# A Mamba-style conv layer on one core: a third conv tap on ScalarE, an accumulating transfer, and ScalarE's products placed behind two decays

## What is computed

```python
# layer 0, DI = 1536 channels, 4 states, R = 48
xs = gn(x) @ in_proj_w.T                       # 768 -> 1536 channels
xs = depthwise_conv3x3(xs, conv_w) + conv_b    # nine taps per channel
u  = xs * sigmoid(xs)
dt, Bs, Cs = split(u @ x_proj_w.T, [R, R + 4])
delta = softplus(dt @ dt_w + dt_b)
dA  = exp(delta[..., None] * A)                # "decays", one per state
dBu = (delta * u)[..., None] * Bs
states = scan(s[t] = dA[t] * s[t-1] + dBu[t])  # along the 4096 positions
y = sum_n(states_n * Cs_n) + D_param * u
y = layernorm(y) * ln_g + ln_b
x = x + y @ out_proj_w.T                       # 1536 -> 768 channels
# layer 1: gn, a 768x768 product, token-statistics attention, a 768x768 product, residual
```

## Time and profile before

| | |
|---|---|
| median of 3 runs | 3728.86 us (3728.01 to 3731.64) |
| the profiled execution: its own time, its span | 3728.46 us, 3726.7 us |
| busy over the span: PE, DVE, ACT, POOL | 3406.2, 2914.2, 2353.8, 2344.5 us |
| 100 to 255 us: conv without scans (PE, DVE, ACT, POOL busy) | 129.75, 81.62, 65.20, 36.70 us of 155 |
| 255 to 2612 us: conv and scans together | 2168.66, 2223.89, 1822.68, 2075.28 us of 2357 |
| 2612 to 2800 us: the tail of layer 0 | 163.86, 123.70, 86.14, 125.30 us of 188 |
| 2800 to 3726.7 us: layer 1 | 893.69, 439.29, 362.81, 104.92 us of 926.7 |

### The profile page before, as it was taken

The page is one execution under the profiler, slowest core; times in us unless marked ns, Lnnn a source line. Parts: engine busy times, 40 slices in busy tenths (PEclk is TensorE's granted clock), DMA queues, the critical chain, the costliest instruction groups (busy, mean ns, idle before and its releaser), DMA issues. The chain is left out here.

```text
span 3726.7 us, 39056 instructions
## 1 busy us (share of the span) xinstructions
PE 3406.2 (91%) x10696; PEld 1733.7 (47%) x10696; DVE 2914.2 (78%) x4082; ACT 2353.8 (63%) x4095; POOL 2344.5 (63%) x1557
## 2 busy tenths in 40 slices
PE   4876799999999999999999999998798999999999
PEld 4432233333333344333333333333235877777787
DVE  4469999999999979999999999999754346566532
ACT  1357777887778757777877778787535556543211
POOL 0149888989889878898988888899850001112211
PEclk7887899999999999999999999999898999999999
DMA  7244455555556544555555555554643223356664
GB/s 284 89 140 109 103 131 139 158 141 146 136 142 157 149 122 122 147 141 140 157 144 146 136 141 150 145 156 113 165 98 115 66 71 111 118 189 211 206 200 153
DMA packets 217034, 529.85 MB, mean 142 GB/s; under 512 B 24728, under 2 KB 45784, under 8 KB 213872
## 3 DMA queue, kind: packets, MB, share of 16 engines
q1 hardware_dynamic: 173808, 376.32, 31.8%
q0 software_dynamic: 43008, 151.02, 18.6%
HBM read 346.11 MB, written 80.48 MB: 114 GB/s over the span
## 5 line engine op out<-in xcount | busy, mean ns | idle before, releaser
L564 PE MATMUL p_in<-xn,win_v 128*128 128x512 f32 (+1 forms) x2304 | 1064.9, 611 | 102.9 <-ACT halo L747 64.6
L580 PE MATMUL p_op<-uy,wout_ring 128*128 128x512 f32 x2160 | 1020.1, 622 | 83.7 <-DVE x_res L952 83.5
L917 DVE TENSOR_TENSOR_SCAN p_da<-p_da,state,g_ring 128x512 f32<-128x512 f32 x672 | 827.1, 1276 | 110.4 <-ACT p_da L706 74.7
L889 POOL TENSOR_TENSOR g_ring<-du,B_bc 128x2048 f32<-128x2048 f32 x192 | 870.6, 4534 | 17.3 <-DMA B_bc<-bc_scratch 2.4
L938 DVE SCALAR_TENSOR_TENSOR p_cv<-win_v,conv_w,p_cv 128x512 f32<-128x512 f32 x960 | 722.7, 753 | 88.0 <-ACT p_cv L768 67.0
L564 PEld LDWEIGHTS p_in<-xn,win_v 128*128 128x128 f32 x2304 | 443.1, 197 | 697.5 <-issue 697.5
L580 PEld LDWEIGHTS p_op<-uy,wout_ring 128*128 128x128 f32 x2160 | 413.4, 198 | 680.4 <-issue 568.3
L706 ACT ACTIVATE p_da<-delta,A 128x512 f32<-128x512 f32 x768 | 499.4, 682 | 12.6 <-ACT state L711 0.2
L923 DVE TENSOR_TENSOR g_ring<-p_da,C_bc 128x512 f32<-128x512 f32 x768 | 486.7, 675 | 0.0
L1366 PE MATMUL banks<-x_split,w_split 128*128 128x512 f32 x1152 | 459.2, 399 | 11.9 <-DVE x_split L1569 6.5
L1368 PE MATMUL banks<-x_split,w_split 128*128 128x512 f32 x1152 | 450.8, 391 | 0.0
(11 more groups left out here) (213 smaller groups left out, 4261.1 us busy)
## 6 DMA issues: line engine op xcount, KB each, us to landing
g_ring<-g_ring POOLq DMA_DIRECT2D x192, 512.0 KB, 5.5
win_v<-in_win SPq DMA_DIRECT2D x192, 384.0 KB, 3.1
wout_ring<-wout_scratch SPq DMA_DIRECT2D x184, 384.0 KB, 4.0
x_ring<-x_scratch SPq DMA_DIRECT2D x192, 256.0 KB, 2.7
q_scratch<-q_ring POOLq DMA_DIRECT2D x96, 256.0 KB, 2.5
x_split<-q_scratch SPq DMA_DIRECT2D x96, 256.0 KB, 3.4
out<-x_ring POOLq DMA_DIRECT2D x96, 256.0 KB, 2.9
x_res<-in_x SPq DMA_DIRECT2D x90, 256.0 KB, 4.6
```

The costliest lines, as they stand in the source:

```text
L564: last = nc.tensor.matmul(p_in[:, 0:n], WR[:, i % NW, t, :], XN[:, t, off:off + n], start=(t == 0), stop=(t == XT - 1))
L580: last = nc.tensor.matmul(p_op[:], OR[:, e % NO, k - h * HALF, :], ucol(c * K + k), start=(k == 0), stop=(k == K - 1))
L889: nc.gpsimd.tensor_tensor(G[:, i % NG], DU[:].unsqueeze(1).broadcast_to([P, NS, N]), BB[:], ALU.mult).then_inc(s_dbu, 1)
L917: nc.vector.tensor_tensor_scan(bank, bank, G[:, i % NG, n, :], init, ALU.mult, ALU.add)\
```

## The change

A third of the conv's products goes from DVE to ACT: tap (2, 0). DVE is left with five taps, three between its two pairs of scans and two at the slot's end. ACT makes three products (`conv_part` has three parts now), and all three stand behind the decays of states 2 and 3, no longer between the centre tap and `keep_state`. POOL adds product 1 onto product 0 with an accumulating transfer in SBUF, which it issues behind the big product with B (L889 of before) once ACT has made product 1 of the tile; its first addition in the next slot waits for that transfer (`s_cf`), and its second one takes product 2. The number of POOL's additions stays. Two semaphores of the layer norm are joined into one, which changes no order. Core of the diff:

```diff
-        CT = sb("conv_part", [P, 2, N])
+        CT = sb("conv_part", [P, 3, N])
@@
-        TAPS = [(dy, dx) for dy in range(3) for dx in range(3) if (dy, dx) not in ((1, 1), (2, 1), (2, 2))]
+        TAPS = [(dy, dx) for dy in range(3) for dx in range(3) if (dy, dx) != (1, 1) and dy < 2]
@@ ScalarE
                 def product(i, n):
-                    wait(act, s_conv, 2 * (i - 1) + n + 1)
-                    nc.scalar.activation(rows(CT[:, n]), win_view(i, 2, 1 + n), ACT.Copy,
-                                         scale=cwt[:, i % K, 7 + n:8 + n]).then_inc(s_ct, 1)
+                    if n == 0:
+                        wait(act, s_conv, 2 * i - 1)
+                    elif n == 1:
+                        wait(act, s_cf, 16 * i)
+                    else:
+                        wait(act, s_conv, 2 * i)
+                    nc.scalar.activation(rows(CT[:, n]), win_view(i, 2, n), ACT.Copy,
+                                         scale=cwt[:, i % K, 6 + n:7 + n]).then_inc(s_ct, 1)
@@
-                    if b is not None:
-                        product(b, 0)
                     i = tile(S, L_SCAN)
                     if i is not None:
                         act.wait_ge(s_du, i + 1)
                         nc.scalar.activation(ucol(i), ucol(i), ACT.Copy, scale=Dp[:, i % K:i % K + 1])\
                           .then_inc(s_skip, 1)
-                    if b is not None:
-                        product(b, 1)
@@
                         decay(i, 2)
                         decay(i, 3)
+                    if b is not None:
+                        product(b, 0)
+                        product(b, 1)
+                        product(b, 2)
                     if S % K == 0 and S < NT:
                         load_norm(S // K)
@@ GpSimd
                     if b is not None:
-                        pool.wait_ge(s_ct, 2 * b + 1)
+                        pool.wait_ge(s_cf, 16 * (b + 1))
                         pool.wait_ge(s_tap, len(TAPS) * (b + 1))
                         nc.gpsimd.tensor_tensor(ucol(b), ucol(b), CT[:, 0], ALU.add).then_inc(s_conv, 1)
-                        pool.wait_ge(s_ct, 2 * b + 2)
+                        pool.wait_ge(s_ct, 3 * b + 3)
                         pool.wait_ge(s_conv, 2 * b + 1)
-                        nc.gpsimd.tensor_tensor(ucol(b), ucol(b), CT[:, 1], ALU.add).then_inc(s_conv, 1)
+                        nc.gpsimd.tensor_tensor(ucol(b), ucol(b), CT[:, 2], ALU.add).then_inc(s_conv, 1)
@@ behind the product with B
+                    t = tile(S, L_CONV)
+                    if t is not None:
+                        pool.wait_ge(s_ct, 3 * t + 2)
+                        nc.gpsimd.dma_start(CT[:, 0], CT[:, 1], accum_op=ALU.add).then_inc(s_cf, 16)
```

19 lines of the change are left out of this document (9 added, 10 removed).

## The result

Four runs of the changed kernel took 3851.54 to 3858.97 us, median **3855.04 us**; four of the kernel before 3728.01 to 3731.64, median 3729.62. The ratio is 1.0336, 95% interval [1.0318, 1.0354]: 125 us slower, where 95 was forecast. That is 32 us above the likeliest value of 3823, and 5 us above the range that the prediction gives its own likeliest case (3795 to 3850). The profiled execution has a span of 3851.2 us.

A forecast was written before the change was run, and what follows sets the result against it. ACT's chain through the table slots was taken as the bound: 5.7 + 2.4 + 2.0 − 3.0 = +7.1 us per chunk, 105 over 14.75 chunks, less 10, so 3728.5 + 95 = 3823 us; 8-in-10 range 3768 to 3868.

The forecast's parts named there:

- A: Likeliest case: ACT's chain sets the Silu and softplus slots, 3795 to 3850 us, chance 0.62.
- rival B: Slower still, through a late landing or a PE clock loss once more per chunk; together chance 0.15.
- B's clock case: PE's idle ahead of the chunk's first input product grows to about 2.8 us; if the clock falls, +2.6 per chunk, 3861.
- What bounds the kernel: In the conv-and-scan stretch, ACT has 0.03 us of room in a Silu slot; its some 33 us lie in six other slots.
- Part 1: Tap taken from DVE: 0.76 us per slot, a gain only where DVE's own work sets the slot's end.
- Part 2: Three products behind the decays take 1.9 us, delaying ACT's chain in Silu and softplus slots; +7.1 us per chunk over all slots.
- The term for the **x_proj slot: Softplus slot with x_proj's copies: products stand in the open behind the decays, 17.32 becomes 19.3 us, +2.0.
- The zero for **slot 1: Chunk's beginning: the norm of x comes 1.9 us later, DVE waits about as long as it gained: 0.
- Part 3: POOL's extra issue costs 0.92 us, its gapless slot goes from 11.94 to 12.86 us, costing the kernel 0.
- Part 4: New transfer lands in an estimated 3.6 us, within the 4.1 us before POOL's first addition, so nothing waits.
- rival B's landing case: Landing takes 5 us or more, POOL sets the pace; at 5.5 us the chunk is 171 and the kernel 3935 us.
- Over the kernel: 14.75 chunks times 7.1 is 105 us, less 5 for the first eight slots and 5 around the second image: +95.

The follow-up runs named there:

- the last run: The kernel before with the third product only in tiles with S mod 4 = 0 or 1, now with two buffers for products 0 and 1: 3701.55 us.

## Why the prediction was right, and where it was short

The mechanism of A was right and accounts for eight of the twelve slots. The number was not A's: the excess of 3.1 us per chunk is mostly PE's lower clock, half of it where rival B had it. The measured time lies outside A's range, and inside the wide one only because B's clock case was let into it.

- **What bounds the kernel.** Right. ACT's chain through the table slots decides, although ACT is the least busy of the four engines in the chunk. Order alone costs 88 us (some 10 of them the clock, an estimate: six chunks at 1.7 us), the tap left out alone brings 48. One reading was wrong: the 33 us are ACT's idle time in all twelve slots; the six slots without a table load hold 25 of them, and the x_proj slot 4.3.
- **Part 1, 0.76 us per slot of DVE, only in some slots.** Right: 0.79 in slots 8 and 9, nothing in the Silu slots. (What moved is one of the nine taps, a sixth of DVE's, not a third of the conv.)
- **Part 2, three products of 1.9 us behind the decays.** Right in Silu and softplus slots: 13.42 against 13.5, 14.42 against 14.5; DVE's waits there are 2.55 and 2.14 against 2.7 and 2.2. The term for the **x_proj slot** was mis-sized: +3.2 instead of +2.0, a wait of 5.62 instead of 4.8. The norm placed first takes 2.4 us off this slot, the products placed in front 2.8, and 0.95 of either is the clock; the two add up to more than 3.2, so they overlap. The zero for **slot 1** was +1.1 (1.5 of clock; without it the slot is 12.6, below the forecast), and the gains in **slots 4 and 5** fell short by 1.0 and 0.4: in slot 4 the low clock reaches on into the out product; slot 5's 0.4 is not the clock.
- **Rival B's clock case came true beside A.** The idle time of PE ahead of the chunk's first input product grew to 2.77 us, forecast as about 2.8, and the clock fell in 8 of the 10 steady chunks (gaps of 2.66 to 2.81 us). I had put a chance of at most 0.15 on that and kept it out of the likeliest case. Its price was too high for the input product (2.6 us forecast, 1.5 measured); that its total of 3861 is near the 3855 measured is in part luck, since the second gap, which the case did not have, makes up for most of it. I had missed the second gap, 2.75 us (0.88 before) ahead of the x_proj slot's second pair of delta products.
- **Part 3, the issue.** POOL's slot is 12.85 us, forecast 12.86, and it costs nothing in the changed kernel, as the run with a third addition shows. The issue waits for ACT's product not only in the x_proj slot but also in slots 1 and 9 (1.5, 1.7 and 0.8 us instead of 2 to 3 in one). The reason given was too strong: "POOL may trail DVE by a few us without holding it" does not hold in kernels whose ACT chain is shorter (+20 us with the issue alone, and 86 us of ACT's waiting in each of the two kernels with all products in front), because ACT's square and next products and DVE's scans wait for what POOL leaves.
- **Part 4, the landing.** 3.3 us median against 3.6 estimated, so rival B's landing case was rightly kept out. The 1.7 us taken as fixed had no row behind it; a line through the two medians (3.3 for 256 KB, 5.5 for 512 KB) gives an estimate of 1.1. The Trainium skill, page "DMA: Bandwidth & Descriptors", section "Anatomy of one DMA — SWDGE (gpsimd) path", gives an estimate of 2.6 us; the trace has 3.2 at the least, so the page does not hold for this transfer. That POOL's first addition would wait for DVE's tap and not for the transfer was wrong: 58.5 us for the transfer against 10.6 for the tap, since the issue itself waits for ACT's second product (44.0 us). The prediction named this as a sign of being wrong; the sign came and, as the run with a third addition shows, costs nothing here.
- **Over the kernel.** From DVE's first scan to the first scan of slot 197 (265.43 to 2758.93, before 262.15 to 2635.01) the kernel grew by 120.6 us, and the first scan came 3.3 later. Cut into 15 stretches of 12 slots from the first scan on, the first grew by 5.3 us, the two in which the second image begins by 0.5 and 4.6, the last by 3.9, and the eleven others by 106, 8.2 to 11.3 each. The deductions for the start and the second image (−10 in all) were of the right kind and too small; the 3.1 us per steady chunk above the forecast, which the filled gap takes back in seven of ten, went the other way and were more.

What stays open: in which chunks a gap costs the clock. 2.15 and 2.16 us of idle time did both in one kernel, and two of the ten gaps in the changed kernel (2.77 and 2.80 us) were harmless. Open too is what the two fixes of the x_proj slot and the norm would bring together; no run has both.

## What to carry to other kernels

Before moving work to the engine that is least busy, lay its chain beside the slot it serves, kind by kind: ACT was idle for 33 us per chunk and had 0.03 us of room in a Silu slot. Place the moved work in the slots that have the room (3704 us) rather than in all (3855 us), and ahead of a table load only if it fits in time that is waited for anyway. When a wait is removed, look for the next thing that the same engines must deliver: three times here (the buffers of the last run, the x_proj slot, the norm) all or part of the time came back one to three slots later.

## What the runs showed of the hardware

The issue of an accumulating transfer takes POOL 0.87 us for 256 KB as for 512 KB (833 to 1036 ns in the new line, rows 12 for the other), against 0.54 for the plain one of 256 KB; the median landing is 5.5 us for 512 KB and 3.3 for 256 KB. Idle times of PE of 2.66 to 2.81 us ahead of the chunk's first input product were followed by a lower clock in 8 of 10 steady chunks (twelve products in 6.9 to 7.1 us instead of 5.39). Useless products kept the clock: with 2.84 us of them in a gap of 2.77, the next twelve products took 5.39 us, and the kernel 16 us less.
